# Five projections of a sequence step as three rounded products each, with a new order of the step

## What is computed

```
u = layernorm(z)
zxbcdt = u @ in_proj_w.T              # 256 gate | 384 x, B, C | 8 dt
xBC = silu(causal_conv4(xBC) + conv_b)
dt = softplus(dt + dt_bias); A = -exp(A_log)
h_t = h_(t-1) * exp(dt*A) + dt*x_t (x) B_t ;  y_t = h_t . C_t + D*x_t
y = rmsnorm(y * silu(z_gate)) ; m = y @ out_proj.T
... residual, layernorm, fc1, gelu, fc2, residual
```

## Time and profile before

| | us |
|---|---|
| median of 3 runs | 4281.23 (4280.12 to 4282.10) |
| the profiled execution: its own time | 4282.0 |
| its span, from the first to the last instruction | 4280.1 |
| mean granted clock of TensorE | 0.974 |
| busy over the span: TensorE, VectorE | 3983.8 (93%), 3492.5 (82%) |
| busy over the span: ScalarE, GpSimd | 3194.4 (75%), 2587.1 (60%) |

### The profile page before, as it was taken

How to read it: one execution, slowest core, us unless ns; L and a number is a source line. 1 busy time by engine, 2 the same in 40 slices (tenths; PEclk the granted TensorE clock), 3 DMA queues, 4 the chain that set the end, 5 groups by cost and what they waited for, 6 DMA issues and landing times.

```text
span 4280.1 us, 95150 instructions
## 1 busy us (share of the span) xinstructions
PE 3983.8 (93%) x31687; PEld 2863.5 (67%) x31687; DVE 3492.5 (82%) x8772; ACT 3194.4 (75%) x4968; POOL 2587.1 (60%) x2713
## 2 busy tenths in 40 slices
PE   7998898799979985799999999999999999999998
PEld 4787578757865885466666666666666666666665
DVE  4568447745775485699999999999999999999997
ACT  4445534553456354699999999999999999999997
POOL 0036103600460056588888888888888888888886
PEclk9999999999989998899999999999999999999999
DMA  2013101400140022111111111111111111111110
GB/s 91 1 53 129 57 2 63 156 20 11 63 164 3 11 72 81 38 41 38 42 39 42 39 42 39 42 39 42 39 39 40 39 42 39 42 39 42 39 42 26
DMA packets 214865, 205.93 MB, mean 48 GB/s; under 512 B 14368, under 2 KB 149152, under 8 KB 214688
## 3 DMA queue, kind: packets, MB, share of 16 engines
q1 hardware_dynamic: 214688, 203.60, 14.6%
HBM read 136.45 MB, written 67.11 MB: 48 GB/s over the span
## 4 chain that ended last, share of the span: by engine, by line
PE 58%; ACT 0%; DVE 0%; POOL 0%; issue 0%; POOLq 0%; DVEq 0%; ACTq 0%
PE g_ps L1043 7%; PE g_ps L1028 6%; PE g_ps L986 6%; PE g_ps L972 5%; PE g_ps L1031 5%; PE g_ps L1060 5%; PE g_ps L1003 3%; PE g_ps L1073 3%; PE g_ps L1079 3%; PE g_ps L1052 3%; PE g_ps L1012 3%; PE g_ps L977 3%; PE g_ps L992 2%; PE g_ps L1068 2%; PE g_ps L965 2%; PE g_ps L997 1%
## 5 line engine op out<-in xcount | busy, mean ns | idle before, releaser
L1355 DVE TENSOR_TENSOR g_mmat<-g_emat,g_ps 128x1024 f32<-128x1024 f32 x512 | 598.9, 1210 | 1.4 <-PE g_ps L1003 1.4
L1194 ACT ACTIVATE g_emat<-g_ps 128x1024 f32<-128x1024 f32 x512 | 521.1, 1024 | 85.7 <-PE g_ps L1031 84.2
L1298 DVE SCALAR_TENSOR_TENSOR g_acc<-g_ps,g_conv_w,g_acc 128x504 f32<-128x504 f32 (+1 forms) x768 | 554.5, 722 | 10.3 <-ACT g_acc L1157 9.9
L873 POOL TENSOR_TENSOR g_acc<-g_acc,g_tap 128x508 f32<-128x508 f32 x384 | 482.5, 1271 | 123.6 <-DVE g_acc L1298 123.6
L613 POOL MEMSET f_s_hi<- 128x192 f32 x4 | 1.0, 258 | 820.7 <-PE f_ps L344 820.7
L1043 PEld LDWEIGHTS g_ps<-g_mmat,g_dtx 128*32 128x32 f32 x8192 | 192.6, 109 | 310.6 <-issue 181.7
L1028 PE MATMUL g_ps<-g_rz,g_l 128*128 128x512 f32 x1024 | 390.0, 462 | 1.6 <-DVE g_z L1383 1.6
L229 PE MATMUL f_ps<-f_s_hi,f_wf_hi 128*128 128x256 f32 x1152 | 360.3, 313 | 5.0 <-DVE f_s_lo L466 5.0
L415 ACT ACTIVATE f_s_hi<-f_ps 128x384 fp32r<-128x384 f32 x256 | 125.7, 491 | 274.0 <-PE f_ps L217 268.9
L1043 PE MATMUL g_ps<-g_mmat,g_dtx 128*32 128x128 f32 x8192 | 329.2, 279 | 0.0
L230 PE MATMUL f_ps<-f_s_lo,f_wf_hi 128*128 128x256 f32 x1152 | 326.2, 283 | 0.0
(11 more groups left out here) (194 smaller groups left out, 12374.3 us busy)
## 6 DMA issues: line engine op xcount, KB each, us to landing
f_xt<-in_x_cols SPq DMA_DIRECT2D x32, 1024.0 KB, 10.3
f_xres<-in_x SPq DMA_DIRECT2D x128, 256.0 KB, 2.8
z<-f_zout SPq DMA_DIRECT2D x128, 256.0 KB, 2.0
g_zin<-z SPq DMA_DIRECT2D x128, 256.0 KB, 2.7
g_zres<-z SPq DMA_DIRECT2D x128, 256.0 KB, 2.9
out<-g_outb SPq DMA_DIRECT2D x128, 256.0 KB, 3.0
f_wf_raw<-in_w_f SPq DMA_DIRECT2D x1, 576.0 KB, 6.9
g_wx<-in_in_proj_t SPq DMA_DIRECT2D x1, 192.0 KB, 2.3
```

The lines of the kernel that those rows point to most:

```text
L873: pool.tensor_tensor(acc[:, j, :, 1:], acc[:, j, :, 1:], tap1[:, j, :, 0:P - 1], ALU.add).then_inc(add_p[j], 1)
L1194: act.activation(emat[:, g, :].rearrange("p (b n) -> p b n", b=2), ps[:, D_BANK[g]:D_BANK[g] + 2, :], ACT.Exp).then_inc(e_a[g], 1)
L1298: dve.scalar_tensor_tensor(out=acc[:, j, :, k:], in0=four(ps[:, bank, :])[:, :, 0:P - k], scalar=conv_w[:, j, 3 - k:4 - k], in1=acc[:, j, ...
L1355: dve.tensor_tensor(mmat[:, g, :].rearrange("p (h n) -> p h n", h=HEADS), emat[:, g, :].rearrange("p (h n) -> p h n", h=HEADS), ps[:, CB, ...
```

## The change

The input-projection weights are loaded as one tile `win_w` and split once into `win_hi` (rounded to fp32r, by ScalarE) and `win_lo` (the rest, by VectorE). In each step ScalarE writes the affine of u twice from the same bank: `ut` in f32 (still used for dt) and `ut_hi` rounded; GpSimd writes `ut_lo = ut - ut_hi`. Each of the five projections becomes three products in fp32r that accumulate: hi by hi, lo by hi, hi by lo. The banks are dealt out anew, and the bodies of all engines are put in a new order. The head of ScalarE's body becomes: affine_u(a_), a call for Silu's table, silu_c(b), silu_x(b, 1), silu_x(b, 0), high_u(a_), absolute(a_), the exponential's table, exp_dt, exps(b, 1), log_dt, exps(b, 0), both taps of part 2, exps(b, 3), exps(b, 2), three taps, affine_h(c), the last tap, then Gelu's table, gelu(c), Silu's table, silu_z(a_, 0), squares(b, 0), squares(b, 1), silu_z(a_, 1), silu_b(a_). VectorE's new order is variance(c), stats_in(p), add_bias(a_), moments_in(p), scale_x(b, 0), residual(c), one_more(a_), stats_mid(c), rounding and positive(a_), moments_mid(c), scale_x(b, 1), step_size(a_), weigh(b, 1), weigh(b, 0), weigh(b, 3), taps(a_, 2, 2), weigh(b, 2), exponent(a_), taps(a_, 1, 2), taps(a_, 2, 3), gate(b, 0), taps(a_, 1, 3), gate(b, 1), high(a_), taps(a_, 0, 2), low(a_), taps(a_, 0, 3), right(a_), finish(c). The bodies of ScalarE (from its middle on) and VectorE are left out of the diff, as are new semaphores and smaller waits.

```diff
-        wx, wz, wdt = sb("wx", [P, 3 * P]), sb("wz", [P, 2 * P]), sb("wdt", [P, HEADS])
+        win_w, wdt = sb("win_w", [P, 5 * P]), sb("wdt", [P, HEADS])
+        win_hi, win_lo = sb("win_hi", [P, 5 * P], FR), sb("win_lo", [P, 5 * P], FR)
         conv_w, conv_b = sb("conv_w", [P, 3, 4]), sb("conv_b", [P, 3])
...
         ps = ctx.enter_context(nc.psum_tensor("g_ps", [P, 8, 512], FP))
-        UT, HT, F1 = 5, 5, 0
-        X_BANK, BC_BANK, Z_BANK = (2, 1), 3, (1, 2)
-        CB, XT_BANK, D_BANK, Y_BANK = 6, (4, 2), (0, 0, 4, 4), (3, 4)
-        SS, OUT, F2 = 6, 5, 3
+        UT, HT, F1 = 1, 3, 0
+        X_BANK, BC_BANK, Z_BANK = (5, 1), 4, (4, 2)
+        CB, XT_BANK, D_BANK, Y_BANK = 6, (5, 5), (0, 2, 2, 0), (2, 6)
+        SS, OUT, F2 = 2, 4, 0
 
...
                 pool.wait_ge(q_d, x.n + 1)
-                held(pool.wait_ge, sqs_p[1], x.n, QUADS)
-                held(pool.wait_ge, sqs_p[0], x.n, QUADS)
-                pool.wait_ge(add_p[1], x.n + 1)
+                pool.wait_ge(add_p[0], x.n + 1)
                 pool.tensor_tensor(l4[64:P], q[64:P, :].bitcast(FP).unsqueeze(1).to_broadcast([64, 4, P]),
                                    ind_g[64:P, :].unsqueeze(2).to_broadcast([64, 4, P]), ALU.mult).then_inc(l4_p, 1)
                 pool.wait_ge(l4_p, x.n + 1)
@@ -901,6 +901,11 @@
                 pool.tensor_tensor(u[:, :, :], uc[:, :, :], r1[:, :].unsqueeze(2).to_broadcast([P, 4, P]),
                                    ALU.mult).then_inc(u_p, 1)
 
+            def low_u(x):
+                pool.wait_ge(ut_a, x.n + 1)
+                pool.wait_ge(uhi_a, x.n + 1)
+                pool.tensor_tensor(ut_lo[:, :], ut[:, :], ut_hi[:, :].bitcast(FP), ALU.subtract).then_inc(ulo_p, 1)
+
...
@@ -921,26 +927,30 @@
 
             def body(at):
                 p, a_, b, c = at(0), at(1), at(2), at(3)
-                if b:
-                    left(b)
                 if c:
-                    add_ffb(c)
-                    root_y(c)
+                    root(c, r2, mv2, mv2_d, r2a_p, r2_p)
+                    norm_h(c)
                 if p:
                     root(p, r1, mv1, mv1_d, r1a_p, r1_p)
                 if c:
                     add_fc2b(c)
-                    root(c, r2, mv2, mv2_d, r2a_p, r2_p)
-                    norm_h(c)
                 if p:
                     norm_u(p)
                 if a_:
                     add_tap(a_, 2)
-                    add_tap(a_, 0)
                     add_tap(a_, 1)
                 if b:
                     add_squares(b, 0)
                     add_squares(b, 1)
+                if a_:
+                    add_tap(a_, 0)
+                    left(a_)
+                if b:
+                    root_y(b)
+                if p:
+                    low_u(p)
+                if a_:
+                    add_ffb(a_)
 
             pipeline(pool, QUADS, body)
 
...
+                held(pe.wait_ge, conv_d[1], x.n * 2, 2 * QUADS)
                 for g in range(4):
                     mm = pe.transpose(ps[:, UT, g * P:(g + 1) * P], u[:, g, :], ident[:, :])
                 mm.then_inc(ut_mm, 1)
 
+            def project(bank, part):
+
+                part = slice(part * P, (part + 1) * P)
+                pe.matmul(ps[:, bank, :], win_hi[:, part], ut_hi[:, :], start=True, stop=False)
+                pe.matmul(ps[:, bank, :], win_lo[:, part], ut_hi[:, :], start=False, stop=False)
+                return pe.matmul(ps[:, bank, :], win_hi[:, part], ut_lo[:, :], start=False, stop=True)
+
             def project_x(x, j):
-                pe.wait_ge(ut_a, x.n + 1)
+                pe.wait_ge(uhi_a, x.n + 1)
+                pe.wait_ge(ulo_p, x.n + 1)
                 if j == 0:
                     held(pe.wait_ge, dtx_d[1], x.n, QUADS)
-                pe.matmul(ps[:, X_BANK[j], :], wx[:, j * P:(j + 1) * P], ut[:, :], start=True, stop=True).then_inc(px_mm[j], 1)
+                if j == 1:
+                    held(pe.wait_ge, e_a[3], x.n, QUADS)
+                project(X_BANK[j], 2 + j).then_inc(px_mm[j], 1)
 
             def project_bc(x):
-                pe.wait_ge(ut_a, x.n + 1)
-                held(pe.wait_ge, fin_d, x.n - 2, QUADS)
-                pe.matmul(ps[:, BC_BANK, :], wx[:, 2 * P:3 * P], ut[:, :], start=True, stop=True).then_inc(pb_mm, 1)
+                pe.wait_ge(uhi_a, x.n + 1)
+                pe.wait_ge(ulo_p, x.n + 1)
+                held(pe.wait_ge, z2_d, x.n - 1, QUADS)
+                project(BC_BANK, 4).then_inc(pb_mm, 1)
 
             def project_z(x, j):
-                pe.wait_ge(ut_a, x.n + 1)
+                pe.wait_ge(uhi_a, x.n + 1)
+                pe.wait_ge(ulo_p, x.n + 1)
                 if j == 0:
-                    held(pe.wait_ge, e_a[1], x.n, QUADS)
-                    pe.wait_ge(conv_d[1], x.n * 2 + 2)
+                    pe.wait_ge(conv_d[2], x.n * 2 + 2)
                 if j == 1:
-                    pe.wait_ge(conv_d[0], x.n * 2 + 2)
-                pe.matmul(ps[:, Z_BANK[j], :], wz[:, j * P:(j + 1) * P], ut[:, :], start=True, stop=True).then_inc(pz_mm[j], 1)
+                    held(pe.wait_ge, gate_d[0], x.n, QUADS)
+                project(Z_BANK[j], j).then_inc(pz_mm[j], 1)
 
             def project_dt(x):
                 pe.wait_ge(ut_a, x.n + 1)
...
@@ -1016,14 +1038,11 @@
                 pe.wait_ge(rz_d, x.n + 1)
                 pe.wait_ge(l4_p, x.n + 1)
                 if g == 0:
-                    held(pe.wait_ge, conv_d[1], x.n * 2 + 4, 2 * QUADS)
+                    held(pe.wait_ge, uhi_a, x.n + 2, QUADS)
                 if g == 1:
+                    held(pe.wait_ge, rsv_d, x.n, QUADS)
+                if g == 3:
                     pe.wait_ge(e_a[0], x.n + 1)
-                if g == 2:
-                    held(pe.wait_ge, z2_d, x.n, QUADS)
-                    pe.wait_ge(dtx_d[0], x.n + 1)
-                if g == 3:
-                    pe.wait_ge(e_a[2], x.n + 1)
                 for half in range(2):
                     pe.matmul(four(ps[:, D_BANK[g] + half, :]), l4[:, g, :], rz[:, 4 * half:4 * half + 4, :],
                               start=True, stop=False)
@@ -1035,8 +1054,8 @@
             def mix(x, g):
                 pe.wait_ge(m_d[g], x.n + 1)
                 pe.wait_ge(dtx_d[g // 2], x.n + 1)
-                if g == 2:
-                    pe.wait_ge(e_a[3], x.n + 1)
+                if g == 0:
+                    pe.wait_ge(e_a[2], x.n + 1)
                 bank, at = Y_BANK[g // 2], (g % 2) * DINNER
                 for h in range(HEADS):
...
@@ -1074,56 +1094,52 @@
 
             def ffn2(x):
                 pe.wait_ge(gl_a, x.n + 1)
-                held(pe.wait_ge, gate_d[0], x.n + 2, QUADS)
                 for g in range(4):
                     mm = pe.matmul(ps[:, F2, g * P:(g + 1) * P], gl[:, g * P:(g + 1) * P], wt[:, 2, :], start=True, stop=True)
                 mm.then_inc(f2_mm, 1)
 
             def body(at):
                 p, a_, b, c = at(0), at(1), at(2), at(3)
+                if c:
+                    sums(c)
+                if a_:
+                    project_dt(a_)
                 if b:
                     turn_x(b, 0)
+                    decays(b, 1)
+                    decays(b, 0)
+                    turn_x(b, 1)
                 if a_:
                     project_bc(a_)
                 if b:
-                    turn_x(b, 1)
-                if a_:
-                    project_dt(a_)
-                if b:
-                    decays(b, 0)
+                    cross(b)
+                    decays(b, 3)
                     decays(b, 2)
-                    cross(b)
-                    decays(b, 1)
-                    decays(b, 3)
                 if a_:
                     project_x(a_, 0)
+                    project_x(a_, 1)
                 if b:
                     mix(b, 0)
                 if c:
                     turn_h(c)
-                if a_:
-                    project_z(a_, 0)
                 if b:
                     mix(b, 1)
+                    mix(b, 2)
                 if c:
                     ffn1(c)
-                if b:
-                    mix(b, 2)
+                if a_:
+                    cumulate(a_)
+                if b:
+                    mix(b, 3)
+                if a_:
+                    project_z(a_, 0)
+                    project_z(a_, 1)
                 if p:
                     turn_u(p)
-                if b:
-                    mix(b, 3)
-                if a_:
-                    project_z(a_, 1)
                 if c:
                     ffn2(c)
-                if a_:
-                    cumulate(a_)
-                if p:
-                    project_x(p, 1)
                 if b:
                     project_out(b)
-                    sums(b)
 
             pipeline(pe, QUADS, body)
...
                 act.activation(vn[:, n, :], vraw[:, n, :], ACT.Square, accum_out=vsq[:, n:n + 1]).then_inc(vsq_ready, 1)
```

(91 more changed lines are left out.)

54 lines of the change are left out of this document (24 added, 30 removed).

## The result

The changed kernel takes **4488.93 us** (median of 4 runs, 4488.32 to 4489.69), the kernel before beside it 4280.67. The ratio is 1.0486 (95% interval 1.0472 to 1.0500): 4.9% slower. The span of the profiled execution is 4487.5 us, the mean granted clock 0.965.

A forecast was written before the change was run, and what follows sets the result against it. A closed ring per step, affine_u to affine_u, bounds the changed kernel: 3.82 + 4.79 + 10.71 + 1.84 = 21.16 us. Growth of 1.58 us over 127 distances adds 201 to 4282.0; forecast 4480 us, range 4389 to 4560.

The forecast's parts named there:

- The superfluous load: Head of ScalarE's body: a call for Silu's table, already loaded, is carried out each step, 1.31 us to the next start.
- The 0.14 for an overlap that the load forbids: ScalarE: affine_u ahead of the load can't overlap it, so 0.81 us from start to start in place of 0.67.
- The two rivals that priced the load at nothing and at twice its length: Superfluous load doesn't run: 4222 us if faster, chance 0.06 in all; it costs its length over again: 4645, chance 0.02.
- The load at the loop's head: Rival: one more table load where ScalarE's loop begins, once for two steps, 83 us more, 4563 us; chance 0.04.
- ScalarE's two additions: high_u (0.67 us) and a fourth table load (1.31 + 0.14) add 2.1 us a step, so ScalarE needs 20.5 us.
- The ring: Closed chain from affine_u to the next affine_u through ScalarE, TensorE, VectorE and ScalarE again, 21.16 us a step.
- the last, 1.84: Ring's closing ScalarE link: squares(1) 0.52, silu_z(1) 0.59, silu_b 0.73 us, then the next affine_u.
- The clock: VectorE idles some 2 us a step, TensorE about as much; neither gap is long, so clock left at 1.00.
- The range: 4389 us (ScalarE's work alone, with 0.1 us a step less) to 4560 (dearer project_bc, hand-overs, head and tail).
- The format: TensorE's projections as three rounded products, 0.75 us against 0.86; five save at least 0.55 us a step, worthless unless ScalarE allows.
- the two ends given: Three rounded products on TensorE: 0.75 us from decay starts, or 1.07 at the dear end from modelled durations.
- What TensorE's relief could give: Kernel before: VectorE has only 0.55 us a step to spare, so relieving TensorE gives at most 70 us in all.

## Why the prediction was right

**The superfluous load is carried out, at 1.31 us with nothing else behind it: right.** The evidence was one load at the end of the old trace. Taken out, 211 us go; added once more, 1.29 us a step with the clock held up. The 0.14 for an overlap that the load forbids isn't shown: without the load silu_c overlaps affine_u no more than the load did. The two rivals that priced the load at nothing and at twice its length are both refuted for this kernel. The second had beside it the drain of the Trainium skill (ScalarE: Activation LUTs, "What ACT_TABLE_LOAD costs"), stated there for a switch to a different set: 2.66 us with the load. The runs show 1.29 to 1.31 us for a load of the set that is there, and of the loads that do switch, that of L1262 in the result's step starts 0.02 us after the activation ahead of it ends, and gelu 1.29 us after the load's start. The load at the loop's head did not come.

**ScalarE's two additions, 20.5 us of work: right within 0.2** (20.28 busy in a common step).

**The ring: right in its links, 0.28 us too long.** Up to cross it took 8.65 us (mine 8.61; inside it turn_x starts 0.11 later than I had it and project_bc is 0.13 longer, the two turn_x and the decays together are 0.20 shorter), up to the end of gate(1) 3005.14 - 2985.83 = 19.31 (mine 19.32; 2985.83 is that step's start, 20.87 ahead of 3006.70). The term that was off is the last, 1.84: from there to the next affine_u it is 1.56. The starts of silu_z(1) and silu_b follow each other by 0.47 and 0.52, where I took 0.59 and 0.73 from the earlier trace rows, distances with a short wait in them (0.02 and 0.09). 127 x 0.28 = 36 us too many.

**The clock: wrong.** "Neither gap is long, so I leave the clock at 1.00" is the step that failed. The pause of 1.45 us before turn_x goes with a fall of the clock in 29 steps, 1.62 us each, 47 us; filling it gives back 45. The two errors, 36 too many and 47 too few, nearly cancel, and the short first distance takes off 5.5: 201 - 36 + 47 - 5.5 = 206.5. That 4480 came within 9 us of 4489 is luck in part; the mechanism of the step was read rightly. The range held either way.

**The format: worth little, as said, at another size.** project_bc takes 0.88 us from its start to that of cross, not 0.75, which is between the two ends given; the pairs of x and z take 0.84 and 0.78 us a projection. Put back to f32, the ring grows by 0.16 us. "The trace shows no group of three that alternates two sets of weights" was an oversight: the spectral half has such groups, of 256 columns, in the trace of before.

```profile
702.62 0.28 PE L229 MATMUL f_ps<-f_s_hi,f_wf_hi 128*128 128x256 f32 x1
702.74 0.28 PE L230 MATMUL f_ps<-f_s_lo,f_wf_hi 128*128 128x256 f32 x1
702.86 0.28 PE L231 MATMUL f_ps<-f_s_hi,f_wf_lo 128*128 128x256 f32 x1
```

At 0.12 us from start to start, three of twice the columns would be estimated at 0.72 us, the cheap end of what was forecast; the row would have shown that the change of weights isn't dear.

**What TensorE's relief could give: half of what I said.** I read 0.55 us a step from VectorE's busy share; with TensorE relieved it was 0.26. VectorE's waits on its own results are part of its queue and not spare time.

**Open.** Why the clock falls in 29 steps and not in more or fewer: cross ahead of project_bc and the f32 products leave the same pause of 1.45 us, and there it falls in 50 and 39, so the pause's length alone doesn't set the number. The kernel without the load, 0.1% faster than before at the edge of what can be measured, is the fastest of those that leave no work out.

## What to carry to other kernels

Before an engine's work is made cheaper, add up the next engines' queues with their waits on their own results: here the second stood 0.26 us behind the first in a step of 19.6, and the third was given more than it had room for. Look in the trace of the old kernel for one case of the thing whose price is in doubt; one superfluous load at its very end decided 200 us. Write the ring down link by link, and move work only where a link gets shorter: filling VectorE's gaps outside it won nothing. And where a new wait makes TensorE pause in every step, put a price on the clock as well as on the pause.

## What was not expected of the hardware

- The granted clock fell to 0.50 behind a pause of 1.45 us that comes in every step, but only in 29 of 126 steps; with a pause of 2.7 us in 118 of 126. With the same 1.45 us in two other versions it fell in 50 and in 39. With six or twelve products that nobody reads in its place it fell in none and in one, and the kernel was 45 and 192 us faster.
- A call for a table that is already loaded costs 1.29 to 1.31 us a step; two calls with no activation between them cost one load (4487.65 against 4488.93 us).
- Three rounded products of 512 columns that alternate two sets of weights took 0.88 us to the start of cross, one f32 product in the same place 0.95.
